# Attention scores from two fp32r parts in 64-row tiles of the array, in place of three bf16 parts in one 96-row tile

## The reference, cut to what matters

```
q = x @ Wq
k, v = jnp.split(ctx @ Wkv, 2, axis=-1)
scores = jnp.einsum('bid,bjd->bij', q, k) * SCALE
probs = jax.nn.softmax(scores, axis=2)
return jnp.einsum('bij,bjd->bid', probs, v)
```

## Time and profile before

| | |
|---|---|
| three runs | 858.06, 856.02, 854.88 us; median 856.02 |
| profiled execution | 851.5 us from its first to its last instruction |
| TensorE matmuls busy | 732.0 us (86%) |
| VectorE busy | 575.9 us (68%) |
| ScalarE busy | 471.2 us (55%) |
| GpSimd busy | 70.4 us (8%) |
| mean granted TensorE clock | 0.945 of full speed |

### The profile page before, as it was taken

How to read it: one execution, slowest core, us unless ns; L and a number is a source line. 1 busy time by engine, 2 the same in 40 slices (tenths; PEclk the granted TensorE clock), 3 DMA queues, 4 the chain that set the end, 5 groups by cost and what they waited for, 6 DMA issues and landing times.

```text
span 851.5 us, 12530 instructions
## 1 busy us (share of the span) xinstructions
PE 732.0 (86%) x4064; PEld 365.9 (43%) x4064; DVE 575.9 (68%) x1030; ACT 471.2 (55%) x918; POOL 70.4 (8%) x63
## 2 busy tenths in 40 slices
PE   0885979999999999999999996647788899999991
PEld 0552522222222222222222343423454688888881
DVE  7783958888888787878888363735557595343357
ACT  0451327777777777777777863025556533332265
POOL 8311100000000000000000020320001011000003
PEclk9998969999999999999999999668889999999995
DMA  8165760030303012030300002222210000000002
GB/s 273 62 219 178 181 246 1 13 89 2 96 3 78 22 40 60 1 99 1 87 14 1 2 19 87 78 78 79 76 39 2 1 1 1 1 1 1 1 1 99
DMA packets 36645, 49.70 MB, mean 58 GB/s; under 512 B 4792, under 2 KB 29688, under 8 KB 35576
## 3 DMA queue, kind: packets, MB, share of 16 engines
q1 hardware_dynamic: 36216, 48.65, 19.0%
q0 software_dynamic: 384, 0.47, 0.3%
HBM read 32.76 MB, written 15.97 MB: 57 GB/s over the span
## 4 chain that ended last, share of the span: by engine, by line
PE 61%; DMA 13%; DVE 9%; SPq 7%; ACT 5%; issue 4%; ACTq 0%; DVEq 0%
PE ps L797 12%; PE ps L784 12%; PE ps L659 10%; SPq L398 6%; DMA stack<-mT 5%; DMA stack<-q_parts 4%; PE ps L958 4%; PE ps L959 3%; PE ps L960 3%; PE ps L633 3%; DMA k_parts<-probs 2%; PE ps L752 2%; PE ps L619 2%; PE ps L974 2%; PE ps L973 1%
## 5 line engine op out<-in xcount | busy, mean ns | idle before, releaser
L1441 DVE TENSOR_REDUCE mm<-ps 128x1 f32<-128x1024 f32 x256 | 301.8, 1219 | 75.5 <-PE ps L659 74.4
L1166 ACT ACTIVATE probs<-ps 128x512 f32<-128x512 f32 x512 | 282.3, 597 | 105.6 <-PE ps L784 102.2
L784 PE MATMUL ps<-stack 99*128 99x512 bf16 x512 | 178.9, 388 | 10.5 <-ACT probs L1166 5.8
L659 PE MATMUL ps<-stack 96*128 96x512 bf16 x512 | 156.5, 386 | 14.6 <-DMA stack<-q_parts 11.7
L797 PE MATMUL ps<-probs,v 128*32 128x512 f32 x1024 | 137.2, 608 | 0.0
L784 PEld LDWEIGHTS ps<-stack 99*128 99x128 bf16 x512 | 42.5, 97 | 191.4 <-ACT probs L1166 173.6
L659 PEld LDWEIGHTS ps<-stack 96*128 96x128 bf16 x512 | 48.7, 99 | 70.9 <-DVE mm L1441 17.7
L551 POOL TENSOR_TENSOR x<-x,rows 128x1024 f32<-128x1024 f32 x12 | 28.3, 2360 | 614.6 <-DVE tok L1411 614.6
L1678 DVE SCALAR_TENSOR_TENSOR k<-ps,cols,early 128x512 f32<-128x512 f32 x32 | 24.0, 750 | 70.1 <-PE ps L960 65.8
L1292 ACT ACTIVATE early<-ps,cols 128x512 f32<-128x512 f32 x32 | 22.1, 690 | 88.3 <-PE ps L960 88.3
L1237 ACT ACTIVATE probs<-ps 96x512 f32<-96x512 f32 x64 | 37.2, 595 | 41.7 <-PE ps L883 41.4
(11 more groups left out here) (142 smaller groups left out, 924.3 us busy)
## 6 DMA issues: line engine op xcount, KB each, us to landing
stack<-q_parts SPq DMA_DIRECT2D x32, 192.0 KB
v_groups<-early SPq DMA_DIRECT2D x8, 512.0 KB, 4.4
stack<-q_parts SPq DMA_DIRECT2D x32, 128.0 KB
v<-v_groups SPq DMA_DIRECT2D x8, 512.0 KB, 13.2
q_parts<-probs SPq DMA_DIRECT2D x8, 384.0 KB, 4.4
k_parts<-probs SPq DMA_DIRECT2D x8, 384.0 KB, 3.0
stack<-k_parts SPq DMA_DIRECT2D x8, 384.0 KB, 4.7
q_parts<-early SPq DMA_DIRECT2D x8, 384.0 KB, 2.6
```

The lines of the kernel that those rows point to most:

```text
L659: mm_ = eng.matmul(ps[:, 2 * i + kh, :], qs[0:ROWS, slot, half, h, P * (t0 + i):P * (t0 + i) + P], stack[0:ROWS, 2 + slot, h, BLK * kh:BLK ...
L784: eng.matmul(ps[:, st_bank(g, k, h), :], stack[0:KROWS, 2 + slot, h, P * kc:P * kc + P], qs[0:KROWS, slot, half, h, :], start=True, stop=T ...
L1166: eng.activation(probs[:, k % 2, h, :], ps[:, st_bank(g, k, h), :], ACT.Exp, scale=SCALE).then_inc(exp_done, 1)
L1441: eng.tensor_reduce(mm[:, half, k:k + 1], ps[:, 2 * i:2 * i + 2, :], AX.XY, ALU.max).then_inc(s_red, 1)
```

## The change

q and k are each cut into two parts, the value rounded to fp32r and the rest rounded to fp32r; `middle`, `low` and their buffers go. A head's stack has 48 rows: q's parts 0, 1, 0 against k's parts 0, 0, 1. Two heads now lie beside each other in the free dimension, and the other two of the group above them, from partition 64 on; a matmul on 48 or 50 rows that start at partition 0 or 64 uses one 64-row tile of the array. `HEADS = (0, 2, 1, 3)` makes successive `scores_t` alternate between the two tiles, and the two tiles of queries of one `scores` are now those of two heads. The maxima are cut in two parts, turned in fp32, and loaded by one DMA for each 64-row tile. The loads of q and k are 16 or 32 rows each, none of them from a broadcast source. In the cross-attention `scores_2` covers two tiles of queries of all four heads in eight matmuls of 78 columns, and its two PSUM banks are filled together, where before a call filled one of two. The ring of parts has 4 slots of the larger size instead of 5.

```
-PARTS = 3
-RING = 5
+TILE_ROWS, HT = 64, 2
+HP = HG // HT
+PARTS = 2
+RING = 4
-ROWS = 6 * DH
+ROWS = 3 * DH
-Q_PART = (0, 0, 0, 1, 1, 2)
-K_PART = (0, 1, 2, 0, 1, 0)
-RUNS = PARTS
+Q_RUNS = ((0, 2), (2, 1))
+K_RUNS = ((0, 1), (1, 2))
+RUNS = HT * len(Q_RUNS)
+HEADS = (0, 2, 1, 3)
...
-            def load_stack(dst, src, heads, which, done):
...
+            def load_stack(dst, src, gg, runs, done):
+
+                for tile in range(HT):
+                    at = HG * gg + HP * tile
+                    for i, n in runs:
+                        rows = src[0:n].rearrange("i (r h) n -> (i r) h n", r=DH)[:, at:at + HP, :]
+                        row = TILE_ROWS * tile + DH * i
+                        eng.dma_start(dst[row:row + DH * n, :, :].bitcast(F32).rearrange("r h n -> r (h n)"),
+                                      rows.rearrange("r h n -> r (h n)")).then_inc(done, 16)
...
+                    rows_i = rows_of(1 - i, ROWS)
                     for kh in range(2):
-                        mm_ = eng.matmul(ps[:, 2 * i + kh, :], qs[0:ROWS, slot, half, h, P * (t0 + i):P * (t0 + i) + P],
-                                         stack[0:ROWS, 2 + slot, h, BLK * kh:BLK * kh + BLK], start=True, stop=True)
+                        mm_ = eng.matmul(ps[:, 2 * i + kh, :], qs[rows_i, slot, half, q, P * t:P * t + P],
+                                         stack[rows_i, 2 + slot, q, BLK * kh:BLK * kh + BLK], start=True, stop=True)
...
-                eng.matmul(ps[:, st_bank(g, k, h), :], stack[0:KROWS, 2 + slot, h, P * kc:P * kc + P],
-                           qs[0:KROWS, slot, half, h, :], start=True, stop=True).then_inc(st_full, 1)
+                tile, q = divmod(HEADS[h], HP)
+                eng.matmul(ps[:, st_bank(g, k, h), :], stack[rows_of(tile, KROWS), 2 + slot, q, P * kc:P * kc + P],
+                           qs[rows_of(tile, KROWS), slot, half, q, :], start=True, stop=True).then_inc(st_full, 1)
...
+                if n >= 1:
+                    eng.wait_ge(s2_red, n)
+                for q in range(HP):
+                    for t in (t0, t0 + 1):
+                        c = CTXE * (2 * q + t - t0)
+                        for tile in range(HT):
+                            mm_ = eng.matmul(ps[:, tile, c:c + CTXE], qs[rows_of(tile, ROWS), slot, half, q, P * t:P * t + P],
+                                             k2[rows_of(tile, ROWS), b, G % GPB, q, 0:CTXE], start=True, stop=True)
...
-                eng.tensor_tensor(rest[:, u % 2, 0:n], ps[:, proj_bank(u), 0:n], part(u)[:, 0, :],
+                eng.tensor_tensor(part(u)[:, 1, :].bitcast(F32R), ps[:, proj_bank(u), 0:n], part(u)[:, 0, :],
                                   ALU.subtract).then_inc(rest_done, 1)
```

More of the change, by code:

```diff
@@ L535, in _ @@
             alone(eng.memset(mpart[:, :, :], 0.0))
-            alone(eng.memset(stack[MROW:MROW + PARTS, 2:4, :, :], 1.0))
-            alone(eng.memset(k2[:, :, :, :], 0.0))
-            alone(eng.memset(k2[MROW:MROW + PARTS, :, :, 0:CTX], 1.0))
+            upper = [slice(TILE_ROWS * tile + 32, TILE_ROWS * tile + 64) for tile in range(HT)]
+            for half in upper:
+                alone(eng.memset(stack[half, 2:4, :, :].bitcast(F32), 1.0))
+            alone(eng.memset(k2[:, :, :, :, :].bitcast(F32), 0.0))
+            for half in upper:
+                alone(eng.memset(k2[half, :, :, :, 0:CTX].bitcast(F32), 1.0))
             alone(eng.memset(v2[:, :, :, :], 0.0))
@@ L880, in scores_t2 @@
                 if n == 0:
-                    eng.wait_ge(m2_in[G % 4], 16 * (G // 4 + 1))
+                    eng.wait_ge(m2_in[G % 4], 16 * HT * (G // 4 + 1))
                 eng.wait_ge(exp_done, 64 * GROUPS + UNITS * G + n - 1)
-                eng.matmul(ps[0:CTXP, ST + h % 2, :], k2[0:KROWS, b, HG * (G % GPB) + h, :],
-                           qs[0:KROWS, Q2_SLOT[G % 4], half, h, :], start=True, stop=True).then_inc(st_full, 1)
+                tile, q = divmod(HEADS[h], HP)
+                eng.matmul(ps[0:CTXP, ST + h % 2, :], k2[rows_of(tile, KROWS), b, G % GPB, q, :],
+                           qs[rows_of(tile, KROWS), Q2_SLOT[G % 4], half, q, :], start=True, stop=True).then_inc(st_full, 1)
             def weigh_2(G, half):
@@ L1065, in high @@
                     eng.wait_ge(part_out[slot], 16 * (u // RING))
-                eng.activation(part(u)[:, 0, :], ps[:, proj_bank(u), 0:n], ACT.Copy).then_inc(hi_done, 1)
-            def middle(u):
-                eng.wait_ge(rest_done, u + 1)
-                eng.activation(part(u)[:, 1, :], rest[:, u % 2, 0:width(u)], ACT.Copy).then_inc(mid_done, 1)
+                eng.activation(part(u)[:, 0, :].bitcast(F32R), ps[:, proj_bank(u), 0:n], ACT.Copy).then_inc(hi_done, 1)
             def values(t):
@@ L1086, in _ @@
                         high(u)
-                    for u in range(PROJ_B0, PROJ_K2):
-                        middle(u)
                 for i in range(TPB):
@@ L1141, in chain @@
                 u = PROJ_2 + 2 * NC * b
-                first = u
                 for blk in (2 * b, 2 * b + 1):
                     turn_copy(ln, blk)
-                    if u > first and n == 0:
-                        middle(u - 1)
                     yield
@@ L1642, in cross_unit @@
             def cross_unit(G, n):
-                if G + 2 < GROUPS:
-                    reduce_2(G + 2, n)
+                if G + 2 < GROUPS and n % 2 == 0:
+                    reduce_2(G + 2, n // 2)
                 if n == 1 and G >= 1:
```

207 lines of the change are left out of this document (84 added, 123 removed).

## The result

The changed kernel takes 956.7 us in the median of four runs, against 857.0 for the kernel before beside it; the two lower runs, 908.9 and 922.4, against all of before give a ratio of 1.069 (95% interval 1.060 to 1.079). It is slower. Its four runs lie far apart: 908.9, 922.4, 991.1 and 992.7 us come with mean granted clocks of TensorE of 0.872, 0.854, 0.755 and 0.754, while before stayed within 0.4%.

The account below looks back on a forecast made before the run. It took the self-attention step to be bound by a 2.88 us loop of latencies and ScalarE's exponentials, not score matmuls. Terms +27 (steps), -20 and -10 (loads), -6 (cross units) made -9: 856.0 to 847 us, range 812 to 879.

Parts of the forecast that it names:

- rival (e): Self-attention steps: the clock falls to half since TensorE has less to do; far over 1000 us; 3%.
- the first steps find the clock up (-2): Start of the self-attention steps: the clock is already up there, worth -2 us within the start's -10.
- signs of being wrong: In the profile after: plain steps at or below 2.88 us, or a queue that still takes 30 us.
- Units of the cross-attention: Cross-attention units: waits of about 11 us go, matmul pace and shape changes cost +6, clock -1; -6 us in all.
- The clock term, "-1": Cross-attention units: -1 us for the clock, within the units' -6.
- Steps of the self-attention: Self-attention: exposed fp32r weight loads +28 us, turn steps +6, slack hidden by a slower step -6; rounded to +27.
- price of 0.10 for a change of shape: TensorE's array: each switch between 128-row and 64-row matmuls costs about 0.10 us.
- The loads: q and k loads without broadcast issue at 0.45 us each: -20 us at the cross-attention's start, -10 in the start.
- (a): Self-attention steps: weight loads stay hidden, the step stays at 2.88 us; 819 us in all; 15%.
- (b): Score matmuls: the two tiles don't run together, a plain step takes 3.14 us; 867 us in all; 17%.
- (c): DMA loads: as slow as before, because the queue and not the broadcast is the cause; about 880 us; 9%.
- (d): Self-attention: score matmuls halve and the stage follows; near 750 us; 4%.

Follow-up runs that it names:

- kernel 5: Changed kernel with a pause of TensorE ahead of its first self-attention step: 879.1, 929.8, 954.4 and 1031.9 us.
- kernel 9: Changed kernel with score matmuls of both attentions over all 128 rows, without 64-row tiles: 843.3 us, ratio 0.987.
- kernel 10: Changed kernel with the operands of all score matmuls, both attentions, read as bf16 in the same 64-row tiles: 807.2 us.
- kernel 1: Kernel before with its rows of parts reordered so that no load repeats a source, nothing else: 806.3 us, ratio 0.944.
- experiment 11: Kernel before with plain loads (806.3 us), every second score matmul of the self-attention left out: 802.1 us.
- kernels 4: Changed kernel with the self-attention's score operands read as bf16 in the same 64-row tiles: 847.1 us.
- 7: Changed kernel with bf16 score operands in 64-row tiles in the self-attention and a pause ahead of the steps: eight runs from 840.8 to 855.0 us.
- 6: Changed kernel with the self-attention's score matmuls over all 128 rows and a pause ahead of the steps: 869.1 and 875.1 us.
- kernel 3: Changed kernel with the self-attention's score matmuls over all 128 rows: 867.2 us.

## Why the prediction was wrong

The stages of four kernels, read as in the table above, in us:

| | start | self-attention | to the cross units | cross units | rest |
|---|---|---|---|---|---|
| 5: after, pause, clock back early | 114.4 | 420.8 | 37.1 | 116.2 | 188.8 |
| 9: after, whole rows in both | 111.4 | 413.8 | 38.5 | 90.3 | 188.3 |
| 10: after, bf16 in both | 108.1 | 393.9 | 36.7 | 78.4 | 188.1 |
| 1: before, plain loads | 113.5 | 390.1 | 38.0 | 76.0 | 186.9 |

*The step that failed is rival (e)*, "The clock falls to half in the steps", at 3%, with the reason that "The steps leave no gap of the size at which the clock fell elsewhere". The sum went the same way: it had no term for a lower clock in the steps, and its start counted on "the first steps find the clock up (-2)". The argument asked whether gaps in the steps would make the clock fall. It fell at their entry, behind a wait of only 0.56 us, and the question was whether the steps bring it back. In the kernel before it fell at the entry as well and was back in 13.7 us (the earlier trace rows shows it in the sixth slice); with fp32r over 48 and 50 rows it took 85. The price was wrong too: a step at half is 4.55, not double. TensorE's bars cover 99% of that stretch, so its own order seems to be the floor there. In the profile after, this is +25.6 of the self-attention (446.4 less the 420.8 of kernel 5); in the runs of 991 and 993 it is about 80 more, by the estimate above. None of the prediction's own signs of being wrong, a plain step of 2.88 or less or a queue of 30 us, looked at the clock, and neither came.

*Units of the cross-attention*, "-6", came out at +22.7. The clock term, "-1", carried it: half for 78 us. The other term, score matmuls at the pace of their weight loads and shape changes at +6, was too small as well: at the full clock, in whole rows, the units are at 90.3, and 14.3 over kernel 1, whose loads are as quick; with bf16 in tiles it is 2.4. What tiles with fp32r cost there at the full clock no run showed, since the clock never was full.

*Steps of the self-attention*, "+27", measured +26.9 in kernel 5. Plain step 3.09 for 3.10, both items 0.10 for 0.11, confirmed from the other side by bf16 in the same tiles. The 0.15 to 0.2 for the steps with `turn_out` and `turn_max` were 0.21 and 0.24 (3.70 and 3.35 against kernel 1's 3.28 and 2.90, less the 0.21 of a plain step). So the steps add 27 and 7, and a slower step hides 7 of it, where the forecast had 28, 6 and 6. Its price of 0.10 for a change of shape doesn't hold in a plain step, where bf16 in tiles puts it at 0.02.

*The loads*, "0.45 us each", were 0.49; the waits for the maxima went. "-20" was -13.8 with the clock at 0.73 in that stretch, "-10" was -6.5.

*The rivals.* (a) falls with the step of 3.09. (b) falls: tiles start together, within 0.01 us, in a step of 3.09, for (b)'s 3.14. (c) falls with 15.56 us for 32 loads. (d) falls with experiment 11: half of the score matmuls left out is worth 4 us.

With the clock aside the sum looks sound, though no run has the change itself at the full clock in both stages. Kernel 9, without tiles, is at 843.3, 10 us under before, close to the -9 of the sum. That is luck in part: its stages are -12, +20, -14 and -3 where -10, +27, -20 and -6 were forecast, and the errors cancel. With kernel 5's steps in place of kernel 9's the span would be about 849, 2 under before, an estimate that lies in the range. The account is then: loads without a broadcast win about 47 us (kernel 1). fp32r in place of bf16 costs 27 in the steps (420.8 against 393.9 in the same tiles), and in the units some 12 (90.3 in whole rows against 78.4 for bf16 in tiles). The clock takes the rest. Two parts, 48 rows and tiles win next to nothing: kernel 10, which has them all in bf16, is at 807.2, kernel 1 at 806.3. Its start is 5 us shorter than kernel 1's, its steps and units 4 and 2 longer.

Open stays why the clock can stay down for so long with fp32r over few rows, when with bf16 over the same rows it comes back soon. Rows between 50 and 128 with fp32r weren't tried. Nor is it shown what ended the half-clock stretches, or what decides how long one lasts in the steps: the runs of one kernel differ by over 100 us.

## What to carry to other kernels

Ask of each changed stage not only whether TensorE's clock falls in it, but whether it would come back once it is down, and read the mean granted clock of every run: a kernel that can't bring it back shows first in runs that lie apart. Before counting matmuls saved, follow the loop of one step; what stands in it is what a change can win or lose, here the weight load behind a wait. When a change rewrites a layout and its loads together, run the loads alone: here they were the whole gain.

## What the runs showed of the hardware

- With score matmuls of fp32r over 48 and 50 rows the granted clock stood at 0.50 for 85, 78 and 109 us in traces, with TensorE's bars covering 95% and more; in one trace (kernel 5) it was back after 10. With bf16 over the same rows the stretch at the steps' entry was 7 and 14 us, with fp32r over 128 rows 7 (kernels 4 and 7, and 6), with bf16 over 96 and 99 rows 14 in the kernel before. In kernels 5 to 7 and in the kernel before, these times hold part of a wait of nearly 5 us.
- An fp32r weight load of 128 columns takes 0.18 to 0.19 us and exposes 0.10 behind a wait; bf16 takes 0.09 to 0.10 and exposes almost nothing, in tiles too. The number of rows makes no difference (184 ns at 50 rows in kernel 5's page, 187 at 128 in kernel 3's).
- A series of 24 loads, of which a third repeat their source three times and a third twice, takes 1.37 us a load to issue, with the 16 DMA engines busy at a share of 0.21; the same bytes by plain loads take 0.46, at 1.00.
- 64-row tiles in place of a full-array shape cost 0.02 us in a plain step of bf16 (2.90 for 2.88), and more in a step with transposes: 0.12 to 0.16 with bf16 (3.40 and 3.06, against kernel 1's 3.28 and 2.90, where `turn_max` is in bf16), 0.21 and 0.19 with fp32r (3.70 and 3.35, against 3.49 and 3.16 in whole rows).
